# Work moved across the stage edges of a three-stage transformer kernel

## What is computed

```python
xn = _layernorm(x, axis=-1)
x = x + _L0_attn_ref(xn, ...) + _L0_ffn_ref(xn, ...)

# ffn: 8 experts, each token goes to its best 2, plus one shared expert
topk_w, topk_idx = jax.lax.top_k(softmax(x @ gate_weight.T), 2)
y = sum over the 2 of topk_w * (silu(x @ w_gate.T) * (x @ w_up.T)) @ w_down.T  +  shared

# attention: 16 heads of 16; causal linear attention and 4 memories
sq = elu(q) + 1
n_f = jnp.einsum('bhsd,mhd->mbhs', sq, fine_memory_norms)
rel = n_f.mean(-1)                       # mean over the sequence
w = jax.nn.softmax(rel, axis=0)          # weight of each memory
out_fine = (outs * w).sum(0)
memory_output = exp_prob * out_fine + (1.0 - exp_prob) * out_coarse
gate = jax.nn.sigmoid(memory_gate)
output = (gate * memory_output + (1.0 - gate) * local_output) @ w_o.T
```

## Time and profile before

| what | us |
|---|---|
| median of 3 runs (lowest, highest) | 646.67 (643.94, 651.8) |
| the profiled execution | 644.98 |
| its span, first to last instruction | 643.2 |
| first matmul of the experts block | 215.20 |
| first matmul of the attention block | 377.46 |
| PE busy | 576.3 (90%) |
| DVE busy | 476.2 (74%) |
| ACT busy | 343.2 (53%) |

### The profile page before, as it was taken

The page is one execution under the profiler, slowest core; times in us unless marked ns, Lnnn a source line. Parts: engine busy times, 40 slices in busy tenths (PEclk is TensorE's granted clock), DMA queues, the critical chain, the costliest instruction groups (busy, mean ns, idle before and its releaser), DMA issues. The chain is left out here.

```text
span 643.2 us, 21856 instructions
## 1 busy us (share of the span) xinstructions
PE 576.3 (90%) x7929; PEld 491.8 (76%) x7929; DVE 476.2 (74%) x1254; ACT 343.2 (53%) x791; POOL 317.7 (49%) x392
## 2 busy tenths in 40 slices
PE   1998999998999599999999969889989998899995
PEld 0786887886888499999999947667767777677773
DVE  3484485484488387777777776979987997889995
ACT  4547648638646244334344435656656665566653
POOL 2047047057055473111010013878886887788885
PEclk9999999999999699999999976989999998999998
DMA  9034734725437343764444442354282426342220
GB/s 311 35 114 171 248 124 186 246 105 199 167 142 282 99 126 126 234 210 140 138 147 131 130 139 71 105 134 137 66 275 62 150 81 233 92 143 85 77 69 34
DMA packets 65036, 92.66 MB, mean 144 GB/s; under 512 B 9556, under 2 KB 49460, under 8 KB 64948
## 3 DMA queue, kind: packets, MB, share of 16 engines
q1 hardware_dynamic: 54644, 69.76, 32.7%
q0 software_dynamic: 8032, 21.12, 10.7%
q10 hardware_dynamic: 2272, 0.53, 0.4%
HBM read 51.13 MB, written 40.24 MB: 142 GB/s over the span
## 5 line engine op out<-in xcount | busy, mean ns | idle before, releaser
L1724 POOL DMA_INDIRECT yg<-d_grouped_y,from_row x64 | 80.4, 1256 | 15.1 <-issue 10.7
L995 ACT ACTIVATE silu<-e_up 128x176 f32<-128x176 f32 x72 | 22.9, 318 | 90.3 <-PE e_up L91 90.3
L1551 ACT ACTIVATE with_mem<-a_ring 128x680 f32<-128x680 f32 (+2 forms) x63 | 46.7, 742 | 19.1 <-PE a_ring L1432 19.1
L89 PE MATMUL e_up<-wb,xb 128*128 x144 | 50.9, 354 | 1.4 <-DVE xb L1018 1.4
L833 POOL TENSOR_TENSOR ticks<-lane 128x1 f32<-128x1 f32 x4 | 2.3, 563 | 92.8 <-DVE slot_i L746 92.8
L91 PE MATMUL e_up<-wb,xb 128*128 x144 | 46.9, 325 | 0.0
L90 PE MATMUL e_up<-wb,xb 128*128 x144 | 46.8, 325 | 0.0
L1575 ACT ACTIVATE attT<-a_ring 128x256 f32<-128x256 f32 x32 | 12.3, 384 | 64.1 <-PE a_ring L1461 64.1
L1672 DVE TENSOR_TENSOR probs<-a_ring,causal_s 128x1024 f32<-128x1024 f32 (+3 forms) x46 | 39.8, 892 | 4.0 <-PE a_ring L1452 3.8
L1032 DVE TENSOR_TENSOR h_sb<-e_up,silu 128x128 f32<-128x128 f32 x72 | 21.0, 292 | 28.3 <-ACT silu L995 20.3
L667 DVE TENSOR_TENSOR silu<-t_u,silu 128x512 f32<-128x512 f32 (+1 forms) x24 | 16.4, 685 | 32.6 <-PE t_u L91 13.5
(11 more groups left out here) (284 smaller groups left out, 2031.8 us busy)
## 6 DMA issues: line engine op xcount, KB each, us to landing
v<-d_rows SPq DMA_DIRECT2D x77, 128.0 KB, 2.1
d_grouped_y<-y_sb SPq DMA_DIRECT2D x73, 128.0 KB, 1.9
d_v<-v_half SPq DMA_DIRECT2D x8, 544.0 KB, 4.1
d_q<-halves SPq DMA_DIRECT2D x8, 512.0 KB, 3.1
d_k<-halves SPq DMA_DIRECT2D x8, 512.0 KB, 3.2
total<-d_base SPq DMA_DIRECT2D x8, 512.0 KB, 4.5
out<-total SPq DMA_DIRECT2D x7, 512.0 KB
v<-d_v SPq DMA_DIRECT2D x6, 544.0 KB, 6.8
```

The costliest lines, as they stand in the source:

```text
L89: pe.matmul(out, a[0], b[0], start=start, stop=False)
L1551: act.activation(with_mem[n % 3][:, :, :].rearrange("p (m q) w -> p q m w", m=KC)[:, lo:hi, :, 0:WN], ring[:, at:at + hi - lo, 0:KC * WN]. ...
L1724: pool.indirect_dma_start(yg[tile % GATHERS][:, k, :], None, d["grouped_y"], bass.IndirectOffsetOnAxis(ap=c["from"][:, k, tile:tile + 1], ...
```

## The change

It has these parts.

- **Tokens, end.** SP reads the four row numbers before it waits for the scatters, into four registers; the four loads follow the wait. ACT calls Silu once after its last Exp, and no longer at the start of the experts block.
- **Experts, last slots.** `SLOTS` is still 72, but the loops of ACT, DVE and SP run 17 passes (68 slots); slots 68 to 71 are written out, and leave out the up projection of slot 71, the transposes of blocks 71 and up, and what ACT and DVE do for them.
- **Memory weights and gates.** POOL sums q and makes `norm_bd` and `of_mean` after its tables; DVE makes the gates before its loop; PE makes the means in slot 69 with two matmuls against `c["before"]` (all ones by then); DVE takes the maximum and the difference in slot 70; ACT calls Exp, then Sigmoid, at the end of its list. In attention only the five operations of `weights` are left, first in DVE's order; `qmean`, `mean` and `mexp` are gone from the orders, and so `mean` from the ring. The memset of `with_mem` goes from DVE to POOL, and the load of `causal` goes to the start of the experts block on SP.
- **Late wait.** SP no longer waits for the stores of `d_grouped_y`; POOL does in attention, after the first scores and before its first gather.
- **Routing tables.** DVE's three operations on `from`, `total_w`, `cw` stand before the last `hb_low`, no longer after the last copy.
- **Places.** `y_sb`, `mw`, the gates and `causal` lie in the third buffer of `halves`, for which DVE and SP wait until its last store has landed.

```diff
 UNROLL = 4
-SLOTS = -(-(NBLK + 1) // UNROLL) * UNROLL
+SLOTS = NBLK + 1
+PASSES = NBLK // UNROLL
+MEAN_AT = PASSES * UNROLL + 1
...
+            sp.wait_ge(s_ready, 1)
+            at = [sp.value_load(c["start"][0:1, j:j + 1], min_val=0, max_val=E * REGION - P) for j in range(UNROLL)]
+            sp.wait_ge(s_tailed, 16 * E)
             for u in range(2):
                 sp.wait_ge(s_sc[u], B // 2 * SCATTERED)
-            sp.wait_ge(s_tailed, 16 * E)
-            sp.wait_ge(s_ready, 1)
             for j in range(UNROLL):
-                at = sp.value_load(c["start"][0:1, j:j + 1], min_val=0, max_val=E * REGION - P)
-                sp.dma_start(c["xg"][j], d["rows"][bass.ds(at, P), :]).then_inc(c["s_ga"][j], 16)
+                sp.dma_start(c["xg"][j], d["rows"][bass.ds(at[j], P), :]).then_inc(c["s_ga"][j], 16)
...
             act.activation(c["keep"][:, :], c["gate"][:, :], ACT.Exp, scale=-1.0)
+            act.activation(tick_s, neg[:, 0:1], ACT.Silu)
...
             fetch(slice(UNROLL, UNROLL + 1), 0)
-            with sp.Fori(0, SLOTS // UNROLL) as it:
+            sp.wait_ge(c["s_hst"][2], late_free)
+            for h in range(2):
+                of = slice(h * CH, (h + 1) * CH)
+                sp.dma_start(c["causal"][of, :], d["causal"][of, of]).then_inc(c["s_causal"], 16)
+            with sp.Fori(0, PASSES) as it:
...
-            sp.wait_ge(s_y, SLOTS + 3)
-            sp.dma_start(grouped_y[SLOTS:SLOTS + 1, :, :].rearrange("i p c -> p (i c)"), y_sb[0][:, :]
-                         ).then_inc(s_yst[0], 16)
-            for q in range(2):
-                sp.wait_ge(s_yst[q], 16 + 8 * SLOTS + (16 if q == 0 else 0))
             for i in range(UNROLL):
-                sp.wait_ge(s_ga[i], 16 * (SLOTS // UNROLL + 1 + (i < 1)))
+                sp.wait_ge(s_ga[i], 16 * (PASSES + 1 + (i < 1)))
+            for slot in range(PASSES * UNROLL, SLOTS + 1):
+                sp.wait_ge(s_y, slot + 3)
+                sp.dma_start(grouped_y[slot:slot + 1, :, :].rearrange("i p c -> p (i c)"), y_sb[slot % 2][:, :]
+                             ).then_inc(s_yst[slot % 2], 16)
...
+                if slot < NBLK:
...
+                if slot + 2 < NBLK:
+                    pe.wait_ge(s_ga[(u + 2) % UNROLL], 16 * (slot // UNROLL) + (16 if u < 2 else 32))
+                    transposed((u + 2) % UNROLL, q)
+                if slot == MEAN_AT:
+                    pe.wait_ge(s_mq, 1)
+                    for m in range(KC):
+                        mm = pe.matmul(ps_mean.rearrange("p (b k n) -> p b k n", b=B, k=KC)[:, :, m, :],
+                                       c["before"][:, :], of_mean[:, m, :, :], start=True, stop=True)
+                    mm.then_inc(s_mean, 1)
...
-            act.activation(tick_s[:, :], c["lane"][:, :], ACT.Silu)
...
+            act.wait_ge(s_mx, 1)
+            act.activation(mw, mw, ACT.Exp, scale=1.0 / SEQ)
+            act.activation(c["tick"], c["lane"][:, :], ACT.Sigmoid)
...
+            dve.wait_ge(c["s_hst"][2], late_free)
+            link(dve.tensor_scalar(over_keep, keep[:, :], 1.0, None, ALU.add))
+            link(dve.reciprocal(gate, over_keep))
+            link(dve.tensor_scalar(keep[:, :], gate, -1.0, 1.0, ALU.mult, ALU.add))
+            link(dve.tensor_scalar(keep[:, :], keep[:, :], 1e-30, None, ALU.max))
+            link(dve.reciprocal(over_keep, keep[:, :]))
...
+            for slot in range(PASSES * UNROLL, SLOTS):
+                n, q, o = slot + 4, slot % 2, (slot - 1) % 2
+                if slot < NBLK:
+                    products(n, q)
+                if slot + 2 < NBLK:
+                    low_tokens(n, q)
+                if slot == MEAN_AT + 1:
+                    dve.wait_ge(s_mean, 1)
+                    link(dve.tensor_reduce(mw_m[:, 0, :, :, :].rearrange("p b g r -> p (b g) r"),
+                                           ps_mean.rearrange("p (g n r) -> p g r n", n=NM, r=2), AX.X, ALU.max))
+                    dve.tensor_tensor(mw.rearrange("p b g n r -> p (b g) n r"),
+                                      ps_mean.rearrange("p (g n r) -> p g n r", n=NM, r=2),
+                                      mw_m[:, 0, :, :, :].rearrange("p b g r -> p (b g) r").unsqueeze(2)
+                                      .broadcast_to([P, B * NP, NM, 2]), ALU.subtract).then_inc(s_mx, 1)
+                result(n, q, 8 * slot + 16 - (8 if q else 0))
+                if slot == SLOTS - 1:
+                    dve.wait_ge(s_tables, 1)
+                    dve.tensor_copy(c["from"][:, :, :], c["slots"][:, :, :])
+                    link(dve.reciprocal(total_w, total_w))
+                    dve.tensor_tensor(c["cw"][:, :, :], c["cw"][:, :, :],
+                                      total_w.unsqueeze(1).broadcast_to([P, TOP, NTA]), ALU.mult)
+                low_hidden(n, o)
...
+            link(pool.tensor_tensor(qtot, c["qsum"][:, :, :, 0], c["qsum"][:, :, :, 1], ALU.add))
+            for m in range(KC):
+                link(pool.tensor_tensor(norm_bd[:, m, :, :, :],
+                                        c["same_head"][:, :].rearrange("p (g r) -> p g r", r=2).unsqueeze(2)
+                                        .broadcast_to([P, PP, NM, 2]),
+                                        c["norms"][:, m, :].unsqueeze(1).unsqueeze(3).broadcast_to([P, PP, NM, 2]),
+                                        ALU.mult))
+            for m in range(KC):
+                link(pool.tensor_tensor(of_mean[:, m, :, :],
+                                        norm_bd[:, m, :, :, :].rearrange("p g n r -> p (g n r)").unsqueeze(1)
+                                        .broadcast_to([P, B, n_mean]),
+                                        qtot[:, :, m].unsqueeze(2).broadcast_to([P, B, n_mean]), ALU.mult))
+            pool.sem_inc(s_mq, 1)
...
-    order = [("norms", 0, 0, 0), ("scores", 0, 0, 0), ("qmean", 0, 0, 0), ("norms", 0, 1, 0),
-             ("mean", 0, 0, 0), ("weights", 0, 0, 0)]
+    order = [("weights", 0, 0, 0), ("norms", 0, 0, 0), ("scores", 0, 0, 0), ("norms", 0, 1, 0)]
...
-                if what == "mexp":
-                    since(act, s_mx, 1)
-                    act.activation(mw[:, :, :, :, :], mw[:, :, :, :, :], ACT.Exp).then_inc(s_mexp, 1)
-                elif what == "rows":
+                if what == "rows":
...
+            for x in with_mem:
+                pool.memset(x[:, :, WN:], EPS).then_inc(s_eps, 1)
+            pool.wait_ge(ready["scores"], 1)
+            for q in range(2):
+                pool.wait_ge(c["s_yst"][q], 16 + 8 * SLOTS + (16 if q == 0 else 0))
...
+        late = c["halves"][:, 2, :, :].rearrange("p k n -> p (k n)")
+        cut = list(itertools.accumulate((0, H, H, B * NP * NM * 2, 2 * B * NP * 2, NH, NH, CH, 1)))
+        part = [late[:, i:j] for i, j in zip(cut, cut[1:])]
+        c["y_sb"], c["gate_s"], c["over_keep"], c["causal"], c["tick"] = part[0:2], part[4], part[5], part[6], part[7]
+        c["mw"] = part[2].rearrange("p (b g n r) -> p b g n r", b=B, g=NP, n=NM)
+        c["mw_m"] = part[3].rearrange("p (i b g r) -> p i b g r", i=2, b=B, g=NP)
+        c["s_yst"], c["s_causal"] = [sem(f"c_yst{q}") for q in range(2)], sem("c_causal")
```

More of the change, by code:

```diff
@@ L864, in experts_phase @@
         hb_low = [sb(f"hb_low{q}", [P, P], F32R) for q in range(2)]
-        y_sb = [sb(f"y_sb{q}", [P, H]) for q in range(2)]
+        y_sb = c["y_sb"]
         ps_x = [bank(f"e_x{q}") for q in range(2)]
@@ L955, in _ @@
                 n, q, o, u = slot + 4, slot % 2, (slot - 1) % 2, slot % UNROLL
[L956 to L970, removed]
+                at_dn = at[0][1]
+                if slot < NBLK:
+                    at_up = at[2][0]
+                    pe.wait_ge(s_xl, n + 1)
+                    pe.wait_ge(s_h, n - 1)
+                    for kc in range(KC):
+                        cols = bass.ds(at_up + kc * E * 2 * F, 2 * F)
+                        mm = three(pe, ps_up[q][:, 0:2 * F], [xb[q][i][:, kc, :] for i in range(2)],
+                                   [w["wb"][i][:, cols] for i in range(2)], kc == 0, kc == KC - 1)
+                    mm.then_inc(s_up, 1)
+                at = at[1:]
+                if slot + 1 < NBLK:
+                    if u == UNROLL - 1:
+                        word = word_of(slot // UNROLL + 1)
+                    at.append(columns(word, (u + 1) % UNROLL + 2))
+                if slot + 2 < NBLK:
[7 more added lines that the diff above has]
+                    mm.then_inc(s_mean, 1)
                 pe.wait_ge(s_h, n)
@@ new lines, in _ @@
+                    low_tokens(n, q)
+                    result(n, q, it * 32 + 16 + (16 if u >= 2 else 0))
+                    low_hidden(n, o)
+            for slot in range(PASSES * UNROLL, SLOTS):
+                n, q, o = slot + 4, slot % 2, (slot - 1) % 2
+                if slot < NBLK:
+                    products(n, q)
+                if slot + 2 < NBLK:
+                    low_tokens(n, q)
+                if slot == MEAN_AT + 1:
```

(21 more changed lines are left out.)

122 lines of the change are left out of this document (50 added, 72 removed).

## The result

The changed kernel has a median of 650.89 us over 12 runs (645.78 to 661.03), the kernel before of 648.09 over 12 (642.65 to 651.8): a ratio of 1.0070, with a 95% interval of 1.0037 to 1.0103. After's longest run, 661.03, was at a lower granted clock (0.943), and the ratio leaves such runs out. That is the same by 2%, and slower by 0.4 to 1.0%. The forecast was 639.0 with 645 as its upper end. The profiled execution of after has a span of 644.2 us and a time of 645.99; it is one of its fastest, 4.9 us under its median, as before's (644.98) is 3.1 under its own.

What follows compares the result with a forecast made beforehand. Three places bound it: PE nearly idle 7.2 us before experts, SP's 1.2 us store wait after them, and attention's 17.2 us first tile. Terms 2.0 + 0.5 + 0.2 + 5.0 = 7.7 us off 646.67 gave 639.0, range 632.5 to 645.

Steps and rivals of the forecast that it cites:

- these places: The edge from tokens to experts, the end of the experts block, and attention's first tile, where all gain was expected.
- the third rival: Slower: PE runs out of instructions at moved places; five more stops of 1.9 eat the gain, six give 650; chance 0.06.
- The sign that the prediction named: The prediction is wrong if PE's waits without a releaser grow well past 6.4 us in attention's scores.
- Register loads, 2.0 off: Tokens to experts: SP's register loads fit into its 3.4 us wait, leaving four issues behind it; bounds 1.1 to 2.7 off.
- Silu, 0.5 off: Start of experts: without the table load, DVE no longer waits 0.54 us for ACT's first `xb`; at least 0 off.
- Hidden additions: Start of experts: DVE's gates, SP's `causal` issues and POOL's operations find slack and cost 0, at most 2 us.
- Last slots, 0.2 off: End of experts: SP's 1.2 us wait goes, 0.3 and 0.75 are added; bounds 1.2 off to 1.5 on.
- Late wait: Start of attention: POOL's wait for the stores ahead of its first gather costs 0.
- First tile, 5.0 off: Attention's first tile, 17.2 to 12.2 us: 0.2 from DVE, 3.55 from the means, 1.29 from table loads; bounds 3.5 to 6.5.
- more than the sum: Rival: PE's clock rises in the first tile, up to 1.5 us, and fewer PE waits give 3 more: 634.5; chance 0.15.

Runs made afterwards that it cites:

- s57: After with 57 more PE instructions, as empty waits at the program's start where PE idles; 0.9926 of before.
- edge23: After with the register-load and Silu edits undone and 57 more PE instructions at PE's start; 0.9946 of before.
- a0: The kernel of after, unchanged, run once more; 1.0083 of before.
- b199: Before with 198 empty PE waits, 100 at PE's start and 98 ahead of the experts; 1.0347 of before.
- quiet: After with attention's output stores and the later batches' base loads cut to 32 of 256 columns; 1.0027, 2.8 us under after.
- edge1: Before with only the register loads moved ahead of SP's waits and Silu's tables ahead of the barrier; 0.9965 of before.
- p57: After with 57 more PE instructions, as empty waits ahead of the experts, where they were not free; 0.9979 of before.
- s28: After with 28 more PE instructions, as empty waits at the program's start; 1.0121 of before.
- s44: After with 44 more PE instructions, as empty waits at the program's start; 1.0037 of before.
- s72: After with 72 more PE instructions, as empty waits at the program's start; 0.9959 of before.
- s90: After with 90 more PE instructions as empty waits, 70 at the start and 20 ahead of the experts; 0.9995 of before.

## Why the prediction was wrong

The step that failed stands at the end of its first part: "In the loop of slots and in the 31 further tiles nothing is changed but the phase of the PSUM ring, so the sum is made of these places." What changed there too is the number of every PE instruction: 57 fewer stand ahead (24 matmuls, their weight loads and nine others, where the prediction counted 26 matmuls). That was the third rival, slower by PE running out of instructions, and it had 0.06; its mechanism is what happened. It was priced by five or six whole stops more. What came was 17 stops at packets' edges for 15 and longer ones, 1.2 us on average for 1.0 and 2.7 at the longest for 1.9, with the lower clock behind some of them, which the price left out. The sign that the prediction named, waits grown well past 6.4 us in the scores, looked at the wrong rows: there they fell to 3.4, and the state sums went from none to 11.2. The Trainium skill ("Runtime: NRT & Kernel Launch", section "Instruction fetch mechanics") has blocks of 256 instructions, and the trace agrees (66 packets); it calls a block's edge mostly hidden. In these tiles 15 of 43 edges cost 0.3 us or more each in before and 17 of 43 in after, together 15.7 and 20.5 us; the measurement decides.

How stops and clock make the time of the 30 tiles, in profiled executions:

| kernel | us | PE's waits without a releaser | at half clock | us less the waits, less half of the half clock |
|---|---|---|---|---|
| before | 231.3 | 15.7 | 12.9 | 209.1 |
| s57 | 231.1 | 16.3 | 12.7 | 208.5 |
| edge23 | 224.2 | 11.4 | 3.4 | 211.1 |
| after | 236.5 | 20.7 | 13.7 | 208.9 |
| a0 | 239.5 | 19.1 | 23.9 | 208.4 |
| b199 | 241.2 | 21.2 | 25.8 | 207.1 |
| quiet | 238.4 | 15.7 | 23.9 | 210.7 |

The last column is the same within 2%, whatever was moved where, and so it is in the profiles of edge1, p57, s28, s44, s72 and s90 (206.9 to 209.9): the tiles themselves did not get slower by more than that. One execution is a sample, though: after and a0 are one program, and differ by 10 us of half clock.

Term by term:

*Register loads, 2.0 off:* 2.56 at the place (SP's end; the first product 2.58), inside the bounds. *Silu, 0.5 off:* nothing: PE's first up projection did not wait for DVE, as the prediction read the row, but for PE's own register load. But of the 2.58 us little reached attention, which starts at 377.22 against 377.46. A piece is the clock: it rises at 220.6 us in after and at 220.9 in before, so from the first product on after has 5.52 us at half clock and before 3.24; half of the difference, 1.1 us, is an estimate of its price. That is a matter of the execution: in a0, the same program as after, the clock rises at 219.2. Another piece is PE's waits for `hb` in the slots, 2.2 us in five against 0.7 in three, behind copies to `y_sb` that waited for a store. Together they come to more than the 2.1 us that were lost up to slot 68. Why the stores landed later in after's slots stays open. In edge1's profile attention starts 1.2 us earlier than before.

*Hidden additions:* hidden; DVE's gate operations end at 216.29, and it still waits 1.40 us for the first Silu. *Last slots, 0.2 off:* 0.2 on, within the bounds: from PE's hidden transposes of slot 68 to attention's first matmul 12.27 us (364.95 to 377.22) against 12.04 (365.42 to 377.46). The last down projection waits 1.86 us for DVE where it waited 1.11, the 0.75 that was forecast. What the sum did not have is the clock, which fell at 374.2 us in after and only at 378.0 in before: that down projection took 1.43 us from its first matmul to its last one's end, against 0.86. *Late wait:* 0, as forecast: POOL's first gather starts 0.7 us later than before (381.82 against 381.14), and no wait of PE in the first tile names it. *First tile, 5.0 off:* 4.26 (17.19 to 12.93), inside the bounds 3.5 to 6.5; the granted clock was 0.50 all through it, against the rival "more than the sum".

The sum was thus 7.7 where s57, with before's numbers in attention, shows 4.8 (2.5 to 7.0): a little too large. The 9.3 us between s57 and after, which the forecast did not have, come with the moved edges; how they divide between the stops and the clock behind them is not shown.

## What to carry to other kernels

On a program that PE runs straight through with many small matmuls, count PE's instructions before and after a change: an edit far away that adds or removes a few dozen can move every later stop; here the same work took up to 2 per cent more or less. When a small change is judged, run it also with some tens of empty instructions in an idle place of that engine, with more than one count, so that its own worth and the shift come apart; and a wait of PE in the midst of equal matmuls that names no releaser is to be looked up in the instruction queue's packets. A good shift is kept only until the next edit.

## What the runs showed of the hardware

In attention instruction packets took 0.88 to 1.85 us to move, and in no profile did PE go on earlier than 0.97 us behind the end of the packet that it needed. PE goes from one packet's edge to the next, 256 instructions, in 3 to 7 us as a rule (128 of them, the `values`, in 0.65 us: 430.17 to 430.82 in after), and a packet starts to move when PE stands 170 to 450 instructions behind 256n and needs it at 449, so the supply is never far ahead. Why a stop is costliest in instructions 176 to 287 of a tile, behind those dense 128, the runs don't settle.

The clock fell to 1.2 GHz at some of the longer stops or just behind them: in before at 425.7, 480.4 and 535.0 us (stops that ended at 425.88, 479.25, 533.76), in after at 442.5, 483.4 and 541.4 (441.57, 482.80, 539.45), for 3.4 or 6.8 us each; behind others of that length it did not (1.88 us at 464.05 and 1.65 at 573.45 in after). The tile above, with a stop of 2.71 us, took nearly 4 us more than the next.

An instruction of two empty waits on PE, on a semaphore that has long been reached, took 0.11 us: (11.34 - 4.92) / 57.
